# Soft mixture: the experts' second products from rounded high and low parts, with the weights fetched per expert and pair

## The reference, cut to what matters

```
logits = einsum('bnd,esd->bnes', x, phi)
dispatch = softmax(logits, axis=1)
combine = softmax(logits over all E*S slots)
slots = einsum('bnd,bnes->besd', x, dispatch)
h = gelu(einsum('besd,edh->besh', slots, w1) + b1)
y = einsum('besh,ehd->besd', h, w2) + b2      # the second product: K = 768, N = 192
out = einsum('besd,bnes->bnd', y, combine)
```

## Time and profile before

| | us |
|---|---|
| median of 3 runs (range) | 961.5 (959.38 to 962.42) |
| the profiled execution's own time | 958.58 |
| its span, first to last instruction | 956.9 |
| PE busy | 872.8 (91%) |
| DVE busy | 473.1 (49%) |
| ACT busy | 459.7 (48%) |
| POOL busy | 180.3 (19%) |
| mean granted TensorE clock | 0.97 |

### The profile page before, as it was taken

How to read it: one execution, slowest core, us unless ns; L and a number is a source line. 1 busy time by engine, 2 the same in 40 slices (tenths; PEclk the granted TensorE clock), 3 DMA queues, 4 the chain that set the end, 5 groups by cost and what they waited for, 6 DMA issues and landing times.

```text
span 956.9 us, 14902 instructions
## 1 busy us (share of the span) xinstructions
PE 872.8 (91%) x5408; PEld 700.7 (73%) x5408; DVE 473.1 (49%) x1013; ACT 459.7 (48%) x937; POOL 180.3 (19%) x257
## 2 busy tenths in 40 slices
PE   2789979888997979999999899998999999998998
PEld 1765766586586658887888659985899669985898
DVE  4887497687757773346555640045201640055001
ACT  5877368458646834325444542434424543433322
POOL 3050022004000012115610340004200340015000
PEclk9999799979987999999999999999999999999999
DMA  7000000001000000001100300000000000000000
GB/s 193 1 27 13 1 11 26 0 0 33 0 1 0 1 27 22 11 12 34 46 1 1 116 1 1 1 17 0 0 0 0 16 0 0 0 16 1 1 1 17
DMA packets 12711, 15.50 MB, mean 16 GB/s; under 512 B 5312, under 2 KB 10560, under 8 KB 12544
## 3 DMA queue, kind: packets, MB, share of 16 engines
q1 hardware_dynamic: 10656, 9.46, 3.2%
q0 software_dynamic: 2016, 5.51, 2.1%
HBM read 13.39 MB, written 1.57 MB: 16 GB/s over the span
## 4 chain that ended last, share of the span: by engine, by line
PE 73%; DVE 16%; issue 6%; ACT 3%; DMA 1%; SPq 0%; DVEq 0%; POOL 0%; ACTq 0%; POOLq 0%
PE ps L221 20%; PE ps L1503 13%; PE ps L1430 6%; PE ps L1518 4%; PE ps L1169 4%; DVE area L273 4%; PE ps L1250 4%; PE ps L1092 3%; PE ps L1072 3%; PE ps L1288 2%; DVE room L577 1%; ACT area L882 1%; PE ps L1052 1%; DVE dstat L742 1%; PE ps L1209 1%
## 5 line engine op out<-in xcount | busy, mean ns | idle before, releaser
L221 PE MATMUL ps<-xs,ws 128*128 128x512 f32 x460 | 128.6, 425 | 13.3 <-DVE xs L500 9.1
L1503 PE MATMUL ps<-area 128*128 128x192 f32 x768 | 127.4, 326 | 0.0
L1503 PEld LDWEIGHTS ps<-area 128*128 128x128 f32 x768 | 124.8, 190 | 2.0 <-issue 0.5
L221 PE MATMUL ps<-ws,wx 128*128 128x512 f32 x480 | 116.2, 397 | 1.3 <-DVE ws L763 1.3
L221 PEld LDWEIGHTS ps<-xs,ws 128*128 128x128 f32 x460 | 88.2, 200 | 32.7 <-issue 8.9
L1020 ACT ACTIVATE area<-ps,bcol 128x512 f32<-128x512 f32 x96 | 65.7, 689 | 86.6 <-PE ps L221 86.6
L221 PEld LDWEIGHTS ps<-ws,wx 128*128 128x128 f32 x480 | 89.2, 188 | 22.8 <-DVE ws L763 3.0
L774 DVE TENSOR_TENSOR area<-ps,area 128x384 f32<-128x384 f32 x32 | 17.9, 558 | 177.8 <-PE ps L1503 177.8
L882 ACT ACTIVATE area<-ps,nm 112x196 f32<-112x196 f32 (+1 forms) x240 | 85.8, 442 | 33.6 <-DVE nm L608 33.6
L412 POOL TENSOR_TENSOR area<-area,dstat 128x512 f32<-128x512 f32 x32 | 33.0, 1042 | 273.8 <-DVE dstat L739 273.8
L608 DVE TENSOR_REDUCE nm<-ps 112x4 f32<-112x784 f32 (+1 forms) x72 | 62.8, 876 | 37.1 <-PE ps L1072 28.0
(11 more groups left out here) (171 smaller groups left out, 1423.8 us busy)
## 6 DMA issues: line engine op xcount, KB each, us to landing
stage<-in_wall POOLq DMA_DIRECT2D x42, 128.0 KB, 2.4
area<-in_w2e SPq DMA_DIRECT2D x1, 2304.0 KB, 8.4
out<-xres SPq DMA_DIRECT2D x4, 384.0 KB, 2.6
xres<-in_x SPq DMA_DIRECT2D x1, 1152.0 KB, 7.3
area<-in_wall SPq DMA_DIRECT2D x2, 512.0 KB, 6.0
area<-in_w2a SPq DMA_DIRECT2D x1, 576.0 KB, 3.8
room<-in_rel SPq DMA_DIRECT2D x4, 128.0 KB, 5.4
xres<-in_x SPq DMA_DIRECT2D x1, 384.0 KB, 3.2
```

The lines of the kernel that those rows point to most:

```text
L221: last = mm(out_, l, r, start=n == 0, stop=n == len(pairs) - 1)
L1503: last = mm(ps[:, 4 + b, s * D:s * D + D], hTd[:, m, b * T + s * P:b * T + s * P + P], w2x[:, e * MC + m, :], start=m == 0, stop=m == MC - 1)
```

## The change

The second products no longer take float32 operands. Gelu now writes float32 into one of three buffers `hf`; DVE copies it into a rounded high part `hh` and subtracts for a low part `low(m)`. The weights of one expert are fetched raw by SP (`raw_w2`, two buffers, k counts experts over all pairs), and POOL splits them (`split_w2`): high and low weights stand side by side, 2 x 192 columns. For each of the four groups of an expert PE runs, for each of six m, one float32r matmul of the high activations with 384 columns (high and low weights) and one of the low activations with 192 columns (high weights). DVE adds the two halves of the result and the bias in two instructions for each group. PE's order is changed too: the first two hidden products of expert e+1 run ahead of the second products of expert e. The transposes of the next pair move from experts 0 and 1 to experts 2 and 3, the second of them in ACT's list now between expert 3's last gelu and the exponentials. The norm's scaling is spread behind experts 0 and 1.

```diff
@@ -84,6 +84,8 @@
             pass
         wx = sb("wx", [P, 4, WALL - CW1], F32R)
+        with nc.sbuf_tensor("xplain", [P, 3, N + P + 4 * QT], F32) as xplain:
+            pass
         xs = sb("xs", [P, 3, N + P + 4 * QT], F32R)
         ident = sb("ident", [P, P])
         wproj = sb("wproj", [P, 2, 2, D])
@@ -100,7 +102,9 @@
         rs = sb("rs", [P, 2, HG])
         cnm = nm.rearrange("p a b -> p (a b)").rearrange("p (a b) -> p a b", b=2)
         AREA = 16640
-        area = sb("area", [P, AREA])
+        with nc.sbuf_tensor("area", [P, AREA], F32) as area:
+            pass
+        rounded = sb("rounded", [P, AREA], F32R)
         ps = ctx.enter_context(nc.psum_tensor("ps", [P, 8, 512], F32))
         def views(spec):
@@ -152,10 +156,20 @@
-        (dd, dt_, _, ct, bc, w2x, b2row) = views([
+        (dd, dt_, _, ct, bc, _, b2row) = views([
             (2, 2, NE * NS), (4, 2, T), (ST * 2,), (ST, N), (N,), (NE * MC, D), (NE, D)])
         yy = area[:, 0:2 * ST * (D + 1)].rearrange("p (b s d) -> p b s d", b=2, d=D + 1)
-        hTd = area[:, 2 * ST * (D + 1):2 * ST * (D + 1) + MC * N].rearrange("p (a b) -> p a b", b=N)
+        hh = rounded[:, 2 * ST * (D + 1):2 * ST * (D + 1) + MC * N].rearrange("p (a b) -> p a b", b=N)
+        W2AT = 4 * NE * NS + 8 * T + 2 * ST + ST * N + N
+        hf = [xplain[:, k, N:2 * N] for k in range(3)]
+        w2f, w2s = (v_[:, W2AT:W2AT + NE * MC * D].rearrange("p (e m h d) -> p e m h d", e=2, m=MC, h=2) for v_ in (area, rounded))
+        def low(m):
+            if m < 4:
+                return ws[:, 3, m * N:m * N + N].rearrange("p (b t) -> p b t", b=2)
+            return ws[:, 2 * m - 8:2 * m - 6, NE * 2 * NS:NE * 2 * NS + T]
         slots = [ws[:, k, 0:NE * 2 * NS] for k in range(3)]
         dstat = sb("dstat", [P, 5, 2 * ST])
         ncm, csum, rcs = (dstat[:, k, :] for k in range(3))
@@ -207,6 +221,8 @@
         d_st, d_sh, d_ss, d_h, d_gelu, d_y, d_ye, d_o, d_res, stored = (
             sem(n) for n in ("d_st", "d_sh", "d_ss", "d_h", "d_gelu", "d_y", "d_ye", "d_o", "d_res", "stored"))
+        d_hh, d_hl, d_yo, ld_b2, w2_hi, w2_lo, ld_w2_even, ld_w2_odd = (
+            sem(n) for n in ("d_hh", "d_hl", "d_yo", "ld_b2", "w2_hi", "w2_lo", "ld_w2_even", "ld_w2_odd"))
         mm = nc.tensor.matmul
@@ -301,9 +317,20 @@
             sp.dma_start(w2l, w2a).then_inc(ld_l2, 16)
             sp.wait_ge(o_res, 1 + 4 * PAIRS)
-            sp.dma_start(w2x, w2e).then_inc(ld_w2, 16)
-            sp.dma_start(b2row, b2r).then_inc(ld_w2, 16)
+            sp.dma_start(b2row, b2r).then_inc(ld_b2, 16)
+            def raw_w2(k):
+                if k >= 2:
+                    sp.wait_ge(d_y, 1 + 4 * (k - 1))
+                sp.dma_start(w2f[:, k % 2, :, 1, :], w2e[:, k % NE * MC:k % NE * MC + MC, :])\
+                    .then_inc((ld_w2_even, ld_w2_odd)[k % 2], 16)
+            for k in range(2):
+                raw_w2(k)
             for it in range(PAIRS):
+                for k in range(NE * it + 2, min(NE * it + 6, NE * PAIRS)):
+                    raw_w2(k)
                 sp.wait_ge(d_res, 1 + NT * (it + 1))
                 sp.dma_start(out[it * N:(it + 1) * N].rearrange("(t p) d -> p t d", p=P),
@@ -417,6 +444,14 @@
                 for s in range(ST):
                     nc.gpsimd.tensor_tensor(ct[:, s, :], ct[:, s, :], bc, ALU.add).then_inc(d_cs, 1)
+            def split_w2(k):
+                pool.wait_ge((ld_w2_even, ld_w2_odd)[k % 2], 16 * (k // 2 + 1))
+                hi, lo = w2s[:, k % 2, :, 0, :], w2f[:, k % 2, :, 1, :]
+                nc.gpsimd.tensor_copy(hi, lo).then_inc(w2_hi, 1)
+                pool.wait_ge(w2_hi, k + 1)
+                nc.gpsimd.tensor_tensor(w2s[:, k % 2, :, 1, :], lo, hi.bitcast(F32), ALU.subtract).then_inc(w2_lo, 1)
             for ph in range(1, 4):
                 for n in range(PAIRS):
                     if ph == 3 and n:
@@ -432,13 +467,20 @@
                         split_chunk(chunk, k1, experts=chunk >= A_CHUNKS, final=chunk == NCHUNK - 1)
                         k1 += 4
                         chunk += 1
+                    if ph == 3:
+                        for k in range(max(0, NE * n - 2), NE * n + 2):
+                            split_w2(k)
             dispatch_combine(PAIRS - 1)
+            for k in range(NE * PAIRS - 2, NE * PAIRS):
+                split_w2(k)
         @block.vector
         def _(dve):
             V = nc.vector
             start_counts(dve, "dve")
+            dve.sem_inc(d_hl, 3)
             def tiles_of(n, tiles):
                 return [xres[:, n * NT + j, :] for j in range(NT)] + ([xedge] if tiles > NT else [])
@@ -763,17 +805,33 @@
                         V.tensor_tensor(slot_cols(slots[2], b, h)[R1:P],
                                         ps[R1:P, bank + 1, :].rearrange("p (e s) -> p e s", e=2),
                                         slot_cols(slots[2], b, h)[R1:P].bitcast(F32), ALU.subtract).then_inc(d_ss, 1)
+                front = it + (3 * PAIRS + 1), it + 1, NT
                 if nxt:
-                    front_norm(it + (3 * PAIRS + 1), it + 1, NT, [(d_st, 1 + 4 * it + 4)])
+                    front_stats(*front)
                 for e in range(NE):
-                    for b in range(2):
-                        dve.wait_ge(d_y, 1 + it * 2 * NE + 2 * e + b + 1)
-                        if e + b == 0:
-                            V.memset(yy[:, :, :, D:D + 1], 1.0)
-                        V.tensor_tensor(yy[:, b, 2 * e:2 * e + 2, 0:D],
-                                        ps[:, 4 + b, 0:2 * D].rearrange("p (s d) -> p s d", d=D),
-                                        b2row[:, e, :].unsqueeze(1).broadcast_to([P, 2, D]), ALU.add).then_inc(d_ye, 1)
+                    for m in range(MC):
+                        n = it * NE * MC + e * MC + m
+                        dve.wait_ge(d_gelu, 1 + n + 1)
+                        if m == 0:
+                            dve.wait_ge(d_y, 1 + it * 4 * NE + 4 * e)
+                        f_ = hf[(e * MC + m) % 3].rearrange("p (b t) -> p b t", b=2)
+                        h_ = hh[:, m, :].rearrange("p (b t) -> p b t", b=2)
+                        V.tensor_copy(h_, f_).then_inc(d_hh, 1)
+                        dve.wait_ge(d_hh, n + 1)
+                        V.tensor_tensor(low(m), f_, h_.bitcast(F32), ALU.subtract).then_inc(d_hl, 1)
+                    if e == 0:
+                        dve.wait_ge(ld_b2, 16)
+                        V.memset(yy[:, :, :, D:D + 1], 1.0)
+                    for g in range(4):
+                        dve.wait_ge(d_y, 1 + it * 4 * NE + 4 * e + g + 1)
+                        y_ = yy[:, g // 2, 2 * e + g % 2, 0:D]
+                        V.tensor_tensor(y_, ps[:, 4 + g % 2, 0:D], b2row[:, e, :], ALU.add).then_inc(d_yo, 1)
+                        dve.wait_ge(d_yo, it * 4 * NE + 4 * e + g + 1)
+                        V.tensor_tensor(y_, ps[:, 4 + g % 2, D:2 * D], y_, ALU.add).then_inc(d_ye, 1)
+                    if nxt and e < 2:
+                        front_scale(*front, range(2 * e, 2 * e + 2), [(d_st, 1 + 4 * it + 4)])
                     if nxt and e == 3:
                         front_split(it + (3 * PAIRS + 1), NT, (d_l, ST * it + ST))
                 for k in range(2):
@@ -1010,15 +1068,17 @@
                         A.activation(slot_cols(slots[2], b, h), ps[:, bank + 1, :].rearrange("p (e s) -> p e s", e=2),
                                      ACT.Copy).then_inc(d_sh, 1)
                 for e in range(NE):
-                    if nxt and e in (1, 2):
-                        front_turned_part(it + (3 * PAIRS + 1), 0, e - 1)
-                    act.wait_ge(d_y, 1 + it * 2 * NE + 2 * e)
                     for m in range(MC):
+                        if nxt and e == 3 and m == 2:
+                            front_turned_part(it + (3 * PAIRS + 1), 0, 0)
                         act.wait_ge(d_h, it * NE * MC + e * MC + m + 1)
-                        A.activation(hTd[:, m, :], ps[:, (e * MC + m) % 4, :], ACT.Gelu_apprx_tanh,
+                        act.wait_ge(d_hl, it * NE * MC + e * MC + m + 1)
+                        A.activation(hf[(e * MC + m) % 3], ps[:, (e * MC + m) % 4, :], ACT.Gelu_apprx_tanh,
                                      bias=bcol[:, E1B + e * MC + m:E1B + e * MC + m + 1]).then_inc(d_gelu, 1)
+                if nxt:
+                    front_turned_part(it + (3 * PAIRS + 1), 0, 1)
                 for s in range(ST):
                     act.wait_ge(d_cs, it * ST + s + 1)
@@ -1480,33 +1540,55 @@
                 for b in range(2):
                     to_slots(b, 1)
-                pe.wait_ge(ld_w2, 32)
                 pe.wait_ge(w_split, NCHUNK - QKV_CHUNKS)
                 pe.wait_ge(d_ss, 1 + it * 4 + 2)
+                def hidden(e, m):
+                    if e == 0 and m == 2:
+                        pe.wait_ge(d_ss, 1 + it * 4 + 4)
+                    pe.wait_ge(d_gelu, 1 + it * NE * MC + max(0, e * MC + m - 3))
```

(55 more changed lines are left out.)

## The result

| | before | after |
|---|---|---|
| median, same chip, us | 962.0 | 1035.4 (1031.7 to 1037.1) |
| ratio to before | | 1.0765, 95% interval 1.0732 to 1.0797 |
| the profiled execution's own time | 958.6 | 1035.6 |
| its span | 956.9 | 1033.9 |
| stage D, from its first fetch's issue to the end | 425.8 | 496.1 |

The change makes the kernel 7.6% slower, 5.4 us above the forecast of 1030 and inside its range. Stage D became 70.3 us longer; the stages ahead of it, whose code is the same, took 6.7 us more in this execution (the point is taken up at the end).

What follows compares the result with a forecast made beforehand. The prediction took PE to bound the experts' part, busy 60.67 of 61.0 us a pair. Its six terms summed to +68.8 on 958.6, giving 1027.4, forecast as a median of 1030; range 978 to 1046.

Steps and rivals of the forecast that it cites:

- Part 1: PE's second products: each float32 matmul of 0.325 us becomes a float32r couple of 0.285; -15.4 us.
- Part 2: Second products: PE stalls for low activations from DVE's new chain of copies and subtractions; +9.6 us.
- Part 3: Experts: POOL's weight splits hold DVE's copies and subtractions, 3.5 us for each of 11 fetches; +37.5 us.
- the lower case: Beside POOL's splits only DVE's copies are held, not its subtractions; the hold term would be 15 us less.
- Part 4: Start of combine: ACT's exponentials come after PE's transpose, no longer under expert 3's second products; +12.3 us over three pairs.
- Part 5: Opening of stage D: POOL splits the first two experts' weights ahead of dispatch_combine and PE waits; +4.8 us (3 to 7).
- Part 6: PE's granted clock falls to 1.2 GHz around 15 waits, 1.3 us each; +20 us (0 to 30).
- DVE isn't held: Rival: DVE's copies and subtractions run beside POOL's splits; +17 us, 979; chance 0.15.
- The balance: Rival: a couple of second products near 0.25 us, no hold, no clock loss; within 0.3%; chance 0.03.
- the faster case: Rival: weight loads hidden in second products, 0.240 us a couple, DVE not held; -2.7 us, 959; chance 0.07.

Runs made afterwards that it cites:

- three orders changed: Changed kernel with POOL's splits after DVE's last low part, ACT's exponentials ahead of its transpose copy, and the first two splits behind POOL's scalings: 952.9 us, ratio 0.9918.
- added matmuls: Changed kernel plus three unread 512-column PE matmuls ahead of each of couples m = 2 to 5, group 0, experts 1 to 3: 1012.9 us.
- late splits: Changed kernel, but POOL splits weights only after DVE's last low part of the expert before, except the first two and each expert 1's: 977.3 us.
- two orders changed: Changed kernel with POOL's splits after DVE's last low part and ACT's exponentials ahead of its transpose copy, opening as in the change: 961.4 us, ratio 1.0014.
- exponentials first: Changed kernel with ACT's eight exponentials ahead of its move of the second transposed part: 1020.3 us, ratio 1.0619.
- The first experiment: The run called late splits: changed kernel with POOL's splits waiting for DVE's last low part of the expert before: 977.3 us, ratio 1.0169.

## Why the prediction was right

The signs held, and the three orders and the clock each had their cause shown by a run of its own. By size only the two smallest terms changed places. In us of stage D, from the runs above:

| part | predicted | measured | from |
|---|---|---|---|
| 1, PE's second products | -15.4 | -14.4 | 16 x (14.63 - 13.73) |
| 2, DVE's chain | +9.6 | +6.1 | three orders changed, less the run without the subtraction |
| 3, the hold | +37.5 | +38.4 | added matmuls 479.1, late splits 440.7 |
| 4, exponentials | +12.3 | +14.2 | late splits 440.7, two orders changed 426.5 |
| 5, opening | +4.8 | +8.1 | 426.5 - 418.4 |
| 6, the clock | +20 | +17.0 | 496.1 - 479.1, the experts alone |
| sum | +68.8 | +69.4 | stage D became 70.3 longer |

By medians the hold is 35.6 and the clock 22.5; their sum, 58, is the firmer number.

That the column adds up is in part its construction: parts 3 to 6 are successive differences between 496.1 and 418.4, and parts 1 and 2 alone are measured apart from them, -8.3 where 418.4 lies 7.4 below before. The single terms were off by 13.6 us taken together and their sum by 0.6. That the errors cancelled so well is luck, though each large term came near.

- **Part 1.** Right. A couple takes 0.286 where the prediction had 0.285, but not by its two addends: inside a stream the next matmul starts 0.20 after a wide one and 0.09 after a narrow one. By the Trainium skill (TensorE: Matmul & The Clock Gate, section on Fast Weight Load) weights of 128 columns load fast if the type isn't FP32. An estimate by it, if float32r counts as another type, is the columns alone, 0.240; 0.286 doesn't agree.
- **Part 2.** Right in mechanism, too large: one m of DVE's chain takes 1.07 us in a row (612.42 to 613.49 in the kernel with three orders changed) and not the 1.15 read from the earlier trace rows; over six that is half a microsecond for each expert. Expert 0 has no stall, where 0.3 was forecast.
- **Part 3.** Right, with 3.3 us a split where 3.5 was taken; of the 38.4 in the table 1.2 are the added matmuls in the last expert, as said above. The profile of the change itself shows the stalls: the first group of an expert, start of group 0 to start of group 1, takes 5.62, 5.65 and 6.10 us in experts 1, 2 and 3 of pair 0, and 1.72 in expert 0. That is 3.9, 3.9 and 4.4 more, and the prediction had 4.0, 4.0 and 4.8. Copy and subtraction are both held; the lower case, the copies alone, is excluded by the 3.02 us subtraction.
- **Part 4.** Right: 2.72 idle and 12.50 against the 10.67 of exponentials first are 4.55 in a pair, where 4.1 was forecast; the combine has a stretch at 0.50, which the prediction had booked under part 6.
- **Part 5.** The mis-sized term, 8.1 for 4.8. The wait is 5.06 us, near the term's 4.8, but the transposes and logits behind it ran at the 1.2 GHz level until 555.87, and the opening costs 8.1 in all. The prediction had 1.3 for this clock in part 6, so some 2 us are missing even so.
- **Part 6.** Right in size, on a narrower count: the 17.0 are the experts alone, and the clock in the opening and the combines stands in parts 5 and 4. Of the 15 waits that the prediction counted 14 were followed by 3.4 or 6.8 us at the 1.2 GHz level.

Of the rivals, "DVE isn't held" is excluded by the trace (3.02 for a subtraction of 0.69). The first experiment shows what it would have been worth: with nothing held the kernel takes 977, where that rival gave 979. The balance and the faster case needed a couple of 0.25 or less.

The forecast had no term for the stages ahead. The first fetch of stage D was issued at 531.1 before and at 537.8 after; in the other kernels, all with the same code up to there, it lay between 530.8 and 535.9. The five kernels that have the late opening lie between 530.8 and 537.8, the five without it between 531.2 and 534.0. In the changed kernels the stretches at 0.50 ahead of stage D sum to 61 to 81 us, against 58 before. Four of the five with the late opening have one of 6.8 us that starts at 529.8 to 532.0, just ahead of stage D; the fifth, whose stage D starts at 530.8, and the five without it have none there. Whether all this is scatter or has to do with the change is open; one profile of each can't tell. So part of the 5.4 us between 1030 and 1035.4 lies outside what was forecast: stage D by itself was forecast to 1.5 us.

## What to carry to other kernels

Before work is handed to POOL, look at what DVE does at that moment: an instruction of each that reads SBUF in a way that needs the shared ports makes a sum and not a maximum, and here one wait on a semaphore, which lets POOL work beside DVE's PSUM additions, brought 58 of 73 us back. A stall of the bounding engine costs more than its length when the clock falls behind it: here 17 to 22 us on top of some 37. And a cut in the bound pays only after the orders around it are right: the cut of 14.4 us was in every one of these kernels, and the first to be faster than before was the one with three orders changed.

## What the runs showed of the hardware that was not expected

- Work added to PE made the kernel faster: 48 groups of three matmuls, most of them in waits, took 22.5 us off by medians and 17.0 off stage D, by keeping the granted clock in the experts at 1.00.
- The clock fell behind short waits too: in expert 1 of pair 0 a wait of 1.62 us, to 606.58, and two of 0.20 and 0.56 stand ahead of and in 6.8 us at 0.50. But two experts alike don't always do the same: in the last pair the first group takes 4.54 us in expert 1 and 4.60 in expert 2, and only the first has such a stretch.
- The hold goes both ways: POOL's copy of 1.15 us took 1.69 behind a DVE subtraction that had started 0.02 us earlier. And it depends on where the operands lie: a DVE TENSOR_TENSOR with a PSUM input took 0.36 beside POOL's 2.67, while one with two SBUF inputs took 3.02.
